# Scores of a windowed and a latent attention on the two row halves of TensorE

## The reference, cut to what matters

```python
Q, K, V = heads(x @ wq), heads(x @ wk), heads(x @ wv)        # 16 heads of 8
# local branch: blocks of 32 queries, keys of the block before and of the own block
base = (j > i) & (j <= i + 32)                               # 32 x 64
blk0 = (block > 0) | (j >= 32)
sc = where(base & blk0, Qb @ Kw.T / sqrt(8), -inf); p = softmax(sc); local = p @ Vw
# remote branch: 8 heads of 8, 64 latents, each the mean over 4 rows (T = 256)
GQ, GK, GV = heads(x @ wgq), heads(pool(x @ wgk)), heads(pool(x @ wgv))
lsc = where(arange(64) <= arange(T) // 4, GQ @ GK.T / sqrt(8), -inf)
rem = softmax(lsc) @ GV @ r_out_w
out = (sigmoid(Q . gate_local) * local + sigmoid(Q . gate_remote) * rem) @ w_out
```

## Time and profile before

| | |
|---|---|
| Median of three runs | 1795.48 us (1791.98 to 1797.09) |
| Profiled execution | 1784.54 us, span 1782.8 us, mean granted PE clock 0.955 |
| PE busy | 1623.9 us (91%) |
| PE weight loads | 1198.6 us (67%) |
| DVE busy | 1143.2 us (64%) |
| ACT busy | 1007.7 us (57%) |
| POOL busy | 832.5 us (47%) |

### The profile page before, as it was taken

How to read it: one execution, slowest core, us unless ns; L and a number is a source line. 1 busy time by engine, 2 the same in 40 slices (tenths; PEclk the granted TensorE clock), 3 DMA queues, 4 the chain that set the end, 5 groups by cost and what they waited for, 6 DMA issues and landing times. The chain is left out here.

```text
span 1782.8 us, 43704 instructions
## 1 busy us (share of the span) xinstructions
PE 1623.9 (91%) x13929; PEld 1198.6 (67%) x13931; DVE 1143.2 (64%) x2695; ACT 1007.7 (57%) x2546; POOL 832.5 (47%) x1413
## 2 busy tenths in 40 slices
PE   4799999999999999989996899999999999995883
PEld 4655555555555555547996688888888888884772
DVE  3356555555555555543443699999999999995661
ACT  3355555555555555543442677777777777762341
POOL 5235555555555555553444444444444444412664
PEclk9999999999999999999998799999999999996676
DMA  7412221222222212212221112112111111115444
GB/s 194 128 31 76 55 55 54 54 54 54 54 54 54 54 54 54 54 47 83 65 65 44 31 43 43 40 38 43 41 40 41 43 40 41 43 35 109 96 84 118
DMA packets 207886, 107.45 MB, mean 60 GB/s; under 512 B 102745, under 2 KB 196250, under 8 KB 207770
## 3 DMA queue, kind: packets, MB, share of 16 engines
q1 hardware_dynamic: 197594, 93.16, 20.9%
q0 software_dynamic: 10240, 13.64, 3.5%
HBM read 61.85 MB, written 40.16 MB: 57 GB/s over the span
## 5 line engine op out<-in xcount | busy, mean ns | idle before, releaser
L662 POOL TENSOR_SCALAR_AFFINE_SELECT probs<-probs 128x512 f32<-128x512 f32 x256 | 183.8, 742 | 157.4 <-ACT probs L1446 157.3
L899 DVE TENSOR_REDUCE mneg<-bankS 128x2 f32<-128x256 f32 x256 | 107.5, 420 | 215.1 <-PE bankS L1778 193.7
L1446 ACT ACTIVATE probs<-bankT 128x1024 f32<-128x1024 f32 x128 | 131.1, 1025 | 180.7 <-PE bankT L1798 180.7
L900 DVE TENSOR_REDUCE mneg<-bankS 128x2 f32<-128x512 f32 x256 | 174.6, 682 | 0.0
L1437 ACT ACTIVATE qT<-bankA,bd 128x256 f32<-128x256 f32 x256 | 107.7, 474 | 89.8 <-PE bankA L1760 89.8
L1760 PE MATMUL bankA<-xnT,wd 128*128 128x256 f32 x512 | 149.6, 416 | 0.0
L655 POOL CAST qb<-qT 128x256 bf16<-128x256 f32 x256 | 97.7, 400 | 95.2 <-ACT qT L1437 95.0
L1812 PE MATMUL bankB<-probs,vaug 128*64 128x512 f32 x512 | 140.2, 626 | 1.1 <-ACT yT L1453 1.0
L1795 PE MATMUL bankT<-qT,kT 37*128 37x512 f32 x512 | 136.7, 610 | 3.5 <-DMA qT<-mT 1.8
L1542 ACT ACTIVATE pe<-pr 128x768 f32<-128x768 f32 x128 | 108.2, 845 | 28.2 <-DVE pr L1240 26.0
L1246 DVE STREAM_TRANSPOSE pt<-pe 128x768 f32<-128x768 f32 x128 | 123.8, 967 | 0.4 <-ACT pe L1542 0.2
(11 more groups left out here) (317 smaller groups left out, 4640.8 us busy)
## 6 DMA issues: line engine op xcount, KB each, us to landing
rzb<-reciprocals SPq DMA_DIRECT2D x128, 128.0 KB
yT<-yT SPq DMA_DIRECT2D x64, 128.0 KB
xtab<-tab SPq DMA_DIRECT2D x32, 192.0 KB, 2.0
xs_sorted<-zeros SPq DMA_DIRECT2D x1, 4608.0 KB, 19.2
qT<-xs_sorted SPq DMA_DIRECT2D x36, 128.0 KB, 2.1
ys_sorted<-qT SPq DMA_DIRECT2D x36, 128.0 KB, 1.8
value_rows<-vrow SPq DMA_DIRECT2D x32, 128.0 KB, 1.8
vx<-value_rows SPq DMA_DIRECT2D x256, 16.0 KB, 1.8
```

What stands on the lines that cost most here:

```text
L662: pool.affine_select(out=blocks, in_=blocks, compare_op=ALU.is_ge, fill=0.0, base=0, pattern=[[0, 4], [1, P]], channel_multiplier=-1).then ...
L899: dve.tensor_reduce(mneg[:, n.half, 0, :, j], bankS[:, :, 0:128], AX.X, ALU.max, negate=True)
L900: dve.tensor_reduce(mneg[:, n.half, 1, :, j], bankS[:, :, 128:384], AX.X, ALU.max, negate=True).then_inc(S["red_done"], 1)
L1446: act.activation(pT[:, g % 2].rearrange("p e j t -> p e (j t)"), bankT[:, 0:2, :], ACT.Exp, scale=SCALE0).then_inc(S["exp_done"], 1)
```

## The change

Each score product takes 64 rows of TensorE in place of 128. Rows 0 to 63 (head groups 0 and 1) write bank 0 of the pair and rows 64 to 127 (groups 2 and 3) bank 1, so bank k now holds the local scores of groups 2k and 2k+1 for both blocks, and in its last 128 columns the latent scores of block 2g+k. To have the latent product on either half, `wgqk` is loaded twice (two more transfers) and `gkm` is copied to all four row groups (two more ACT copies a batch). The masks of a half, 384 columns, are laid out once in `masks` and enter by one bf16 product a half, with `pick1` (four 32x32 identities) as weights. `attend` reads `pt` by the new layout, with the same number of products. `pick1` and `masks` are cleared by POOL and filled by twenty ACT copies before the first round, for which PE now waits; `passed(pe)` is one semaphore increment on PE's sequencer.

```diff
@@ -224,6 +224,8 @@
         wsum = sb("wsum", [P, 2, 2])
         carry = sb("carry", [E1, 2, 1])
         mxs = sb("mxs", [P, 2, 12])
+        pick1 = sb("pick1", [P, 4, W], BF16)
+        masks = sb("masks", [P, NB // 2, 6, NL], BF16)
         pr = sb("pr", [P, 2, 12 * NL])
         pe1 = sb("pe1", [P, 2, 2, 12, W])
         pt = sb("pt", [P, NB // 2, 2, 2, 6, W])
@@ -395,7 +397,8 @@
             sp.wait_ge(S["zeroed1"], 2)
             for k, w in enumerate(("wq", "wk")):
                 sp.dma_start(wqk[:, k, :], a["L1_attn_" + w]).then_inc(S["w1_in"], 16)
-                sp.dma_start(wgqk[:, k, 0:DL], a["L1_attn_" + ("wgq", "wgk")[k]]).then_inc(S["w1_in"], 16)
+                for h in range(2):
+                    sp.dma_start(wgqk[:, k, h * DL:(h + 1) * DL], a["L1_attn_" + ("wgq", "wgk")[k]]).then_inc(S["w1_in"], 16)
                 sp.dma_start(gcol[:, k:k + 1], a["L1_attn_gate_" + ("local_w", "remote_w")[k]].rearrange("h (d o) -> (h d) o", o=1)).then_inc(S["w1_in"], 16)
             for h in range(4):
                 sp.dma_start(wv[:, 32 * h:32 * (h + 1)].rearrange("c (g d) -> c g d", d=8),
@@ -747,6 +750,8 @@
                                  quadcol[:, 0:4 * 8:8].unsqueeze(1).to_broadcast([P, 4 * NB, 4]))
                 pool.tensor_copy(gvx[:, :, :, DL:PW].rearrange("p u k h -> p (u k) h"),
                                  quadcol[:, 0:4 * 8:8].unsqueeze(1).to_broadcast([P, 4, 4]))
+                pool.memset(pick1[:, :, :], 0.0)
+                pool.memset(masks[:, :, :, :], 0.0)
                 pool.memset(cnt_all[:, 0:1], 0.0)
                 pool.memset(carry[:, :, :], 0.0).then_inc(S["pads"], 16)
 
@@ -1165,7 +1170,7 @@
             for u in range(2):
                 dve.sem_inc(S[f"res_out{u}"], 16)
                 dve.sem_inc(S[f"tab_out{u}"], 16)
-            dve.wait_ge(S["w1_in"], 16 * 18)
+            dve.wait_ge(S["w1_in"], 16 * 20)
             dve.wait_ge(S["l1_consts"], 1)
             dve.wait_ge(S["pads"], 64)
             for k in range(2):
@@ -1580,9 +1585,9 @@
                     act.copy(gvx[q, n.half, :, 0:DL].rearrange("p k (g h d) -> p k g h d", h=4, d=8)[:, :, :, h, :],
                              bank[2][q, 320:320 + 2 * DL].rearrange("p (k g h d) -> p k g h d", k=2, h=4, d=8)[:, :, :, h, :])
                 spread(gqx[:, n.half], bank[2][:, 0:T])
-                for g in range(2):
+                for g in range(4):
                     q = slice(W * g, W * g + W)
-                    ins = act.copy(gkm[q, n.half, g, :], bank[2][q, 256:256 + NL])
+                    ins = act.copy(gkm[q, n.half, g % 2, :], bank[2][q, 256:256 + NL])
                 ins.then_inc(S["gk_sb"], 1)
 
             def route(n):
@@ -1660,6 +1665,16 @@
             act.sem_inc(S["gate_sb"], 1)
             act.sem_inc(S["rows_sb"], 1)
             act.wait_ge(S["wprep"], 1)
+            for k in range(2):
+                q = slice(DL * k, DL * k + W)
+                act.copy(pick1[q, :, :], identb[q, q].unsqueeze(1).to_broadcast([W, 4, W]))
+                act.copy(masks[q, 0, 0:2, :], maskl[q, 0, :].unsqueeze(1).to_broadcast([W, 2, NL]))
+                act.copy(masks[q, 0, 2:4, :], maskl[q, 1, :].unsqueeze(1).to_broadcast([W, 2, NL]))
+                for g in range(1, NB // 2):
+                    act.copy(masks[q, g, 0:4, :], maskl[q, 1, :].unsqueeze(1).to_broadcast([W, 4, NL]))
+                for g in range(NB // 2):
+                    ins = act.copy(masks[q, g, 4:6, :], maskr[q, 2 * g + k, :].unsqueeze(1).to_broadcast([W, 2, NL]))
+            ins.then_inc(S["l1_consts"], 1)
             xt1(Batch(0, 0))
             step1(None, Batch(0, 0), Batch(0, 1))
             step1(Batch(0, 0), Batch(0, 1), Batch(1, 0), False)
@@ -1987,13 +2002,20 @@
                     pe.wait_ge(S["s2_ps"], b.b * 4 + g)
                 if g >= 2:
                     pe.wait_ge(S["sub_done"], b.b * 4 + (g - 1))
+                s = (bankS, bankT)[g % 2]
+                half = [slice(DL * k, DL * (k + 1)) for k in range(2)]
+                passed(pe)
                 for k in range(2):
-                    n = 2 * g + k
-                    s = (bankS, bankT)[g % 2][:, k, :]
-                    pe.matmul(s[:, 0:4 * NL], identb[:, :], maskl[:, min(n, 1), :].unsqueeze(1).to_broadcast([P, 4, NL]), start=True, stop=False)
-                    pe.matmul(s[:, 0:4 * NL], qx[:, u, n].rearrange("p h q -> p (h q)"), km[:, u, :, n * W:n * W + 2 * W], start=False, stop=True)
-                    pe.matmul(s[:, 4 * NL:6 * NL], identb[:, :], maskr[:, n, :].unsqueeze(1).to_broadcast([P, 2, NL]), start=True, stop=False)
-                    ins = pe.matmul(s[:, 4 * NL:6 * NL], gqx[:, u, n].rearrange("p h q -> p (h q)"), gkm[:, u, :, :], start=False, stop=True)
+                    pe.matmul(s[:, k, 0:6 * NL], pick1[half[k]].rearrange("p h q -> p (h q)"), masks[half[k], g].rearrange("p s c -> p (s c)"),
+                              start=True, stop=False, skip_group_check=True)
+                for c in range(2):
+                    n = 2 * g + c
+                    for k in range(2):
+                        pe.matmul(s[:, k, c * 2 * NL:(c + 1) * 2 * NL], qx[half[k], u, n].rearrange("p h q -> p (h q)"),
+                                  km[half[k], u, 2 * k:2 * k + 2, n * W:n * W + 2 * W], start=False, stop=True, skip_group_check=True)
+                for k in range(2):
+                    ins = pe.matmul(s[:, k, 4 * NL:6 * NL], gqx[half[k], u, 2 * g + k].rearrange("p h q -> p (h q)"), gkm[half[k], u, :, :],
+                                    start=False, stop=True, skip_group_check=True)
                 ins.then_inc(S["s2_ps"], 1)
 
             def xt1(n, prior):
@@ -2065,10 +2087,10 @@
                 for n in range(2 * g, 2 * g + 2):
                     if n:
                         for k in range(2):
-                            pe.matmul(slots_ps[DL * k:DL * (k + 1), n, 0:PW], pt[:, g, 0, n % 2, 2 * k:2 * k + 2, :].rearrange("p g q -> p (g q)"), vx[:, u, n - 1, k, :],
+                            pe.matmul(slots_ps[DL * k:DL * (k + 1), n, 0:PW], pt[:, g, 0, k, 2 * (n % 2):2 * (n % 2) + 2, :].rearrange("p g q -> p (g q)"), vx[:, u, n - 1, k, :],
                                       start=True, stop=False, skip_group_check=True)
                     for k in range(2):
-                        pe.matmul(slots_ps[DL * k:DL * (k + 1), n, 0:PW], pt[:, g, 1, n % 2, 2 * k:2 * k + 2, :].rearrange("p g q -> p (g q)"), vx[:, u, n, k, :],
+                        pe.matmul(slots_ps[DL * k:DL * (k + 1), n, 0:PW], pt[:, g, 1, k, 2 * (n % 2):2 * (n % 2) + 2, :].rearrange("p g q -> p (g q)"), vx[:, u, n, k, :],
                                   start=(n == 0), stop=True, skip_group_check=True)
                 for k in range(2):
                     for n in range(2 * g, 2 * g + 2):
@@ -2149,6 +2171,7 @@
                     remote(b)
 
             pe.wait_ge(S["wprep"], 1)
+            pe.wait_ge(S["l1_consts"], 2)
             xt1(Batch(0, 0), False)
             step1(None, None, Batch(0, 0), Batch(0, 1))
             step1(Batch(0, 0), None, Batch(0, 1), Batch(1, 0))
```

## The result

| | before | after |
|---|---|---|
| median | 1796.28 us (1791.98 to 1798.07, four runs) | 1775.09 us (1771.46 to 1785.13, four runs) |
| ratio | | 0.9894, 95% interval 0.9846 to 0.9942 |
| profiled execution | 1784.54 us | 1785.13 us |
| stage of layer 1's attention in it | 640.09 us | 622.26 us |
| period of a batch | 19.165 us | 18.507 us |

The prediction was 1773 us (1763 to 1789), 22.3 us faster. The timed median moved by 21.2 us.

What follows compares the result with a forecast made beforehand. DVE's own work plus one wait a batch for `xT` from PE was taken as the bound. Thirty rounds at 0.75 us (-22.5) and the start (+0.2) gave -22.3, hence 1773 us; range 1763 to 1789 for 8 in 10.

Steps and rivals of the forecast that it cites:

- The path: PE ahead of DVE's `xT` wait: of four score groups a batch only `scores(n, 1)` counts, at most 0.84 us.
- The group: One group of scores on PE, halves streaming at once, entry and exit included: 1.0 us against 1.75.
- The seam: Between two batches, from `scores(n, 1)` through turns and copy to `xp`: gain of 0.75 us a batch.
- The wait left: DVE's wait for `xT` before `xp`: 0.09 us a batch remains after the change.
- ACT's copies at nothing: Two more `gkm` copies, 0.40 us a round on ACT, cost nothing, covered by gaps before `attend(b, 2)` and `soft(b, 3)`.
- The start: Start of layer 1: turns 2.3 us and first scores 2.7 later, first two groups 4.0 for 6.5; net +0.2 us.
- The sum: Whole kernel: 30 rounds at 0.75 us give -22.5, start +0.2, together -22.3 us.
- The time itself: Profiled 1784.54 us becomes 1762.2; the timed runs lie some 11 us higher, so 1773 us.
- Less overlap: Rival, score groups on PE: weight loads show, a group takes 1.3 us, gain 13.5, time 1782 us; chance 0.12.
- Failing cover: Rival, ACT's chain from `xT` to `soft(b, 3)`: the added copies cost up to 12.4 us, time 1786; chance 0.10.
- No overlap: Rival, score groups on PE: halves don't overlap, a group takes 1.9 us, time 1803 us, slower; chance 0.05.
- The clock: Rival, PE's new pauses lower the clock: 12.8 us per batch affected, three batches give 1811 us; chance 0.07.

Runs made afterwards that it cites:

- e2: Changed kernel with only score group 1 on halves, groups 0, 2 and 3 on full rows; 1772.64 us, ratio 0.9882 to the kernel before.
- e3: Changed kernel with score groups 0, 2 and 3 on halves, group 1 on full rows; 1791.95 us, ratio 1.001 to the kernel before.
- The second profile: The changed kernel run and profiled once more, nothing altered; 1771.59 us, ratio 0.9906 to the kernel before.
- e1: Changed kernel with each group's products issued all of one half, then all of the other; 1788.22 us, ratio 0.998 to the kernel before.
- e7: Changed kernel without the two added `gkm` copies, latent keys on rows 64 to 127 left at zero; 1775.95 us.
- e6: Changed kernel with four more ACT copies a batch, of the size of those of `gkm`, into a tile nobody reads; 1837.8 us.
- e4: Changed kernel with the turns `xt1(m)` ahead of `shared_down` on PE and their ACT copy ahead of `shared_result`; 1763.16 us, ratio 0.9833 to before.
- e9: e4 with `km` and `gkm` each made by two scaled ACT copies over 128 rows, not four over 32; 1761.27 us, ratio 0.9851 to before.

## Why the prediction was right, step by step

- **The path (right).** "Only `scores(n, 1)`" counts: e2 and e3 show it. One reading beside it was not right: DVE takes up group 0 "only after that work and `invert1`". It was held by PE there, and group 0 on halves took 0.13 us off DVE's work; no gain came of it, since DVE then waits for `xT`.
- **The group (1.0 predicted; 1.09 measured).** From product to product it is 0.94 us. The change to halves shows in front of it, 0.10 more until its first product starts, and the way back behind it, 0.05 more from the turns to the copy. Four f32 passes of `km`, two on each half, went at some 0.22 us, as the earlier trace rows had it.
- **The seam (gain 0.75 predicted, 0.66 measured).** The prediction had 2.87 us from `shT` to `xp`: 0.14 to the start of `shared_down`, then 0.91, 1.0, 0.42, 0.40. It measured 2.96: 0.05, 1.09, 0.94, 0.47, 0.41. The first two together are 1.14 for 1.05, the change to halves; the turns' way to the copy is 0.05 longer. So the term that was sized too small is the price of a group with its entry and exit, 1.09 us for 1.0. PE's new pause before `shared_down` is no part of it: e3 has that pause and the 3.62 us of before.
- **The wait left (0.09 predicted, 0.31 measured).** 0.09 is the longer seam; the other 0.13 is that DVE's own work between `shT` and `xp` became 2.65 us from 2.78, by its maxima of group 0. The prediction took this work as fixed.
- **ACT's copies at nothing (right, with less slack than said).** 0.09 us is left, not 0.24: ACT's keys now begin 0.19 us later after `xp`.
- **The start (+0.2 net predicted; -0.7 measured to the second `xp`).** Its parts were off: turns +1.5 for +2.3 and first scores +2.0 for +2.7, because ACT's copies run beside POOL's normalising where the prediction put them in a row before PE (their own length was 4.8 us for 5.7); the first two groups took 3.65 us for 4.0.
- **The sum.** The prediction took 30 x 0.75; the stage has 29 steady intervals at 0.65, -18.95, and around them -0.7, +0.8 and +1.1, together -17.8. The second profile has -21.0, and the medians moved by -21.2 and -17.7. The forecast of -22.3 is a little more than any of these.
- **The time itself (partly luck).** To come from the profile to a median the prediction added the 11 us by which before's profile lay under its runs. That distance is scatter: after's profile lies 10 us above its median, and the second one 9 below. With medians of after at 1775.09 and 1771.59, that 1773 came within 2 us says less than the period does.
- **The rivals.** Less overlap: e1 shows what it would have looked like (a gain of 0.28 us a batch in place of 0.66, ratio 0.998). Failing cover: out by e7. No overlap: out. The clock: rightly on the list, and wrongly priced. It also fell without pauses of "several us": behind one of 2.19 us in two of four profiles, and with 2.5 to 2.7 us in each batch of e6.

## What to carry to other kernels

Before a product is made faster, find the one consumer that waits at the end of its chain and see which of the products is in front of it: here one group of four carried the whole gain, and moving the consumer's own small product ahead of the queue gave as much with no new layout. An engine freed on one side of a semaphore stands still on the other. The pause of 0.66 us before `shared_down` cost nothing here; the longer ones before `attend(b, 0)` took the clock down in some profiles, and in each batch of e6. A product that is off the path may still hold an engine for a time too short for the waits view, as group 0 held DVE. Measure such a change by a period inside the stage it touches, since whole executions of one kernel differed by 19 us here.

## What the runs showed of the hardware

- f32 products of 64 rows and 128 columns on the two row halves overlap even with a new set of weights for each pass: a group of eight products took 0.94 us in alternating order, 1.33 one half after the other, 1.75 for the same work in full rows. The change from full rows to halves cost 0.10 us, and the turns behind the halves came 0.05 us later to their copy.
- PE took a product of one half ahead of earlier ones of the other half (e1), where the program has them the other way.
- A start of PE after a pause of 0.66 us cost the path nothing: 3.62 us from `shT` to `xp` with it (e3) and without it (before).
- Pauses of PE of 1.2 to 1.9 us in each batch left the granted clock at 1.00 in after and e4. Behind one of 2.19 us it fell to 0.50 for 3.4 us in after and e3, and did not in the second profile of after and in e4, so the length of one pause does not tell. With 2.5 to 2.7 us in each batch it fell in each (e6), though PE was at work in 84% of the stage. Four products in the pause kept it at 1.00.
- ACT's price for these copies is by instruction rather than by rows: four copies of 32 x 64 took 0.83 us, two of 128 x 64 took 0.54 (e9).
